# A decoder layer's quantised feed-forward: 12 of 32 recomputed hidden tiles go through DRAM instead

## What is computed

```python
def _quant_per_tensor(x):
    scale = jnp.maximum(jnp.max(jnp.abs(x)), MIN_RANGE) / QP
    return (_ste_round(x / scale), scale)
def _qlinear(x2d, w, b):
    xq, sx = _quant_per_tensor(x2d)
    wq, sw = _quant_per_tensor(w)
    return (jnp.matmul(xq, wq.T) + b[None, :]) * (sw * sx)
h = _qlinear(x, w1, b1)      # 8192 tokens x 1024
h = gelu(h)
o = _qlinear(h, w2, b2)      # 8192 tokens x 256
```

## Time and profile before

| | us |
|---|---|
| runs: median (lowest to highest of 3) | 1675.04 (1672.29 to 1675.15) |
| the profiled execution, its own time | 1671.48 |
| its span in the trace | 1669.4 |
| end of the last maximum of the first pass, in the span | 1561.66 |
| one pair of groups of the second pass | 23.93 |
| mean granted clock, share of full speed | 0.983 |

### The profile page before, as it was taken

The page is one execution under the profiler, slowest core; times in us unless marked ns, Lnnn a source line. Parts: engine busy times, 40 slices in busy tenths (PEclk is TensorE's granted clock), DMA queues, the critical chain, the costliest instruction groups (busy, mean ns, idle before and its releaser), DMA issues.

```text
span 1669.4 us, 51921 instructions
## 1 busy us (share of the span) xinstructions
PE 1573.6 (94%) x16058; PEld 1401.0 (84%) x16058; DVE 1461.2 (88%) x6184; ACT 1060.9 (64%) x2205; POOL 1051.2 (63%) x1168
## 2 busy tenths in 40 slices
PE   6799999999999999999999999999999999778898
PEld 5689999999999999999999999999999998644465
DVE  4889999999999999999999999999999996679876
ACT  4456666666666666666666666666666666469875
POOL 4557777777777777777777777777777776621000
PEclk9999999999999999999999999999999999789999
DMA  6000000000000000000000000000000000221155
GB/s 211 8 15 29 28 28 28 25 28 28 28 27 22 26 28 28 28 28 28 28 28 28 28 28 22 22 28 28 25 28 28 28 28 17 90 85 51 60 178 166
DMA packets 77732, 71.01 MB, mean 43 GB/s; under 512 B 6272, under 2 KB 77184, under 8 KB 77696
## 3 DMA queue, kind: packets, MB, share of 16 engines
q1 hardware_dynamic: 76736, 70.41, 13.4%
q10 hardware_dynamic: 960, 0.13, 0.1%
HBM read 45.36 MB, written 25.17 MB: 42 GB/s over the span
## 4 chain that ended last, share of the span: by engine, by line
PE 73%; DVE 14%; ACT 6%; issue 4%; POOL 1%; DMA 0%; ACTq 0%; DVEq 0%; SPq 0%; POOLq 0%
PE banks L111 21%; PE banks L112 18%; PE banks L113 18%; PE banks L868 5%; DVE tile_max L2010 4%; PE banks L848 3%; PE banks L892 3%; DVE xn L1241 3%; PE banks L1901 2%; ACT normed L1106 2%; DVE x L1390 1%; DVE ctx_t L1274 1%; ACT ctx_t L1076 1%; DVE kept L2022 1%; PE banks L747 1%
## 5 line engine op out<-in xcount | busy, mean ns | idle before, releaser
L589 POOL TENSOR_TENSOR shifted<-scores,score_max 128x512 f32<-128x512 f32 x256 | 266.9, 1043 | 200.6 <-DVE score_max L1286 159.9
L595 POOL TENSOR_TENSOR exp_t<-exp_copy,exp_t 128x512 f16<-128x512 f32 x256 | 302.5, 1182 | 60.6 <-ACT exp_copy L1091 60.6
L1286 DVE CUSTOM_DVE_ANT_0 scores<-banks,mask 128x128 f32<-128x128 f32 x1024 | 235.0, 286 | 11.6 <-issue 6.0
L1076 ACT ACTIVATE q_t<-banks 128x512 f16<-128x512 f32 x128 | 76.5, 598 | 224.0 <-PE banks L113 224.0
L581 POOL TENSOR_TENSOR v_nat<-kv_copy,v_nat 128x512 f16<-128x512 f32 x124 | 138.8, 1130 | 105.2 <-ACT kv_copy L1079 105.2
L111 PE MATMUL banks<-ctx_t,cross_Wk 128*128 128x256 f32 x512 | 154.7, 302 | 21.8 <-DVE ctx_t L1274 18.5
L1089 ACT ACTIVATE exp_t<-banks 128x512 f16<-128x512 f32 x256 | 155.9, 609 | 6.2 <-PE banks L113 3.8
L1091 ACT ACTIVATE exp_copy<-banks 128x512 f32<-128x512 f32 x256 | 158.6, 620 | 0.0
L868 PE MATMUL banks<-ident,shifted 128*128 128x128 f32 x1024 | 153.8, 279 | 3.9 <-POOL shifted L589 2.8
L111 PE MATMUL banks<-xn_t,cross_Wq 128*128 128x256 f32 x512 | 153.1, 299 | 2.7 <-POOL cross_Wo L269 1.6
L1079 ACT ACTIVATE kv_copy<-banks 128x512 f32<-128x512 f32 x248 | 150.9, 608 | 0.0
(11 more groups left out here) (261 smaller groups left out, 5661.8 us busy)
## 6 DMA issues: line engine op xcount, KB each, us to landing
x_in<-in_x_dram SPq DMA_DIRECT2D x32, 256.0 KB, 2.8
ctx_in<-in_ctx_dram SPq DMA_DIRECT2D x32, 256.0 KB, 2.7
x_residual<-x SPq DMA_DIRECT2D x64, 128.0 KB, 1.7
x_normalised<-normed SPq DMA_DIRECT2D x32, 256.0 KB, 2.1
shared<-x_normalised SPq DMA_DIRECT2D x8, 1024.0 KB, 5.3
shared<-x_residual SPq DMA_DIRECT2D x16, 512.0 KB, 3.8
out_dram<-shared SPq DMA_DIRECT2D x16, 512.0 KB, 2.9
mask<-in_fside_Bx1xSxS_dram SPq DMA_DIRECT2D x64, 64.0 KB, 1.8
```

What stands on the lines that cost most here:

```text
L589: pool.tensor_tensor(shifted[:, q % 2], scores[:, q % 2], score_max[:, q % 2, :].unsqueeze(2).to_broadcast([P, QUAD, P]), ALU.subtract).th ...
L595: pool.tensor_tensor(exp_t[:, q % 2, LO], exp_copy[:, q % 2], exp_t[:, q % 2, HI], ALU.subtract).then_inc(exp_split, 1)
L1076: op = act.activation(hilo(dst, *at)[HI], src, ACT.Copy)
L1286: op = dve.tensor_tensor_reduce(scores[:, q % 2, h, :], sc_bank(q)[:, tile(h)], mask[:, b, :], 1.0, NEG, ALU.add, ALU.max, score_max[:, q ...
```

## The change

Of the recomputed groups k = 3, 5 and 7 the rows t = 1, 3, 5, 7 (12 units, 6 MB) are no longer computed again. The first pass writes them to one of four tiles `held`, and SP stores each to DRAM. In the second pass, where the unit was due, PE does nothing for it, ACT issues the load of the unit into its slot in place of the Gelu, and `round_up` waits for the load. `held` lies in `shared` behind `x_load`: its four tiles cover rows 4 to 7 of the odd half of `h_q` and both `x_again`. So the first two reloads of residuals wait for all maxima and all stores, and so do the first takes of a recomputed group that write there (k = 1, row 4 on ACT and row 5 on DVE). The ring's tiles are now given in the order of the units that still pass through it, and the first three Gelus of the second pass wait for all 64 maxima, where each waited for the maximum of its own tile before.

```diff
@@ feed_forward: which tiles, and where they stand
+    HELD = 4
+    on_dram = lambda k, t: again(k) and k > 1 and t % 2 == 1
+    DRAM_UNITS = [(k, t) for k in range(GROUPS) for t in range(ET) if on_dram(k, t)]
+    AGAIN_UNITS = [(k, t) for k in range(GROUPS) for t in range(ET) if again(k) and not on_dram(k, t)]
+    first_pass = lambda k, t: SEQUENCE[k] * ET + t
+    held_of = {first_pass(*u): m for m, u in enumerate(DRAM_UNITS)}
+    ring_of = {first_pass(*u): m for m, u in enumerate(AGAIN_UNITS)}
+    unit_dram = nc.dram_tensor("hidden_units", (len(DRAM_UNITS), P, TOK), F32, kind="Internal").ap()
...
+    held = shared[:, SLOTS * GB * D:].rearrange("p (n s) -> p n s", n=HELD)
...
+    WAITS_FOR_DRAM = [next(u for u in all_units if u[0] == 1 and u[1] >= ET // 2 and on_act(*u) == act) for act in (True, False)]
...
         if j == 0:
-            at = (UNITS + t) % RING
-            return ring[:, at:at + 1, :] if t < RING else kept[:, t - RING:t - RING + 1, :]
+            return ring[:, t:t + 1, :] if t < RING else kept[:, t - RING:t - RING + 1, :]
...
+    def written(n):
+        if n in held_of:
+            return held[:, held_of[n] % HELD, :]
+        return ring[:, ring_of[n] % RING, :] if n in ring_of else kept[:, n, :]
+
+    def all_on_dram(eng):
+        for m in range(HELD):
+            eng.wait_ge(to_dram[m], 16 * (len(DRAM_UNITS) // HELD))
@@ sync: 12 stores, then the first reloads
+        for m, u in enumerate(DRAM_UNITS):
+            sp.wait_ge(h_ready, first_pass(*u) + 1)
+            sp.dma_start(unit_dram[m], held[:, m % HELD, :]).then_inc(to_dram[m % HELD], 16)
         sp.wait_ge(xt_full, PARTS * GROUPS)
         sp.wait_ge(b2_ready, 3)
+        sp.wait_ge(h_seen, UNITS)
+        all_on_dram(sp)
         reload(0)
@@ tensor: second pass
-            if due(step):
+            if due(step) and not on_dram(*due(step)):
                 k, t = due(step)
-                n = k // 2 * ET + t
+                n = AGAIN_UNITS.index((k, t))
@@ scalar: first pass
-                if g >= KEPT and n >= KEPT * ET + RING:
-                    act.wait_ge(h_seen, n - RING + 1)
-                gelu(kept[:, n, :] if g < KEPT else ring[:, n % RING, :], u1_bank(n), n, t, u_full, h_ready)
+                if n in held_of and held_of[n] >= HELD:
+                    m = held_of[n] - HELD
+                    act.wait_ge(to_dram[m % HELD], 16 * (m // HELD + 1))
+                    act.wait_ge(h_seen, first_pass(*DRAM_UNITS[m]) + 1)
+                if n in ring_of and ring_of[n] >= RING:
+                    act.wait_ge(h_seen, first_pass(*AGAIN_UNITS[ring_of[n] - RING]) + 1)
+                gelu(written(n), u1_bank(n), n, t, u_full, h_ready)
@@ scalar: take, and the second pass
+            if (k, t) == WAITS_FOR_DRAM[0]:
+                all_on_dram(act)
...
                 if j == 0 and t < RING:
-                    act.wait_ge(h_seen, UNITS - RING + t + 1)
+                    act.wait_ge(h_seen, UNITS)
...
-                gelu(unit(k, t)[:, 0, :], u2_bank(j * ET + t), j * ET + t, t, u2_full, h2_ready)
+                if on_dram(k, t):
+                    m = DRAM_UNITS.index((k, t))
+                    if m < HELD:
+                        act.wait_ge(to_dram[m], 16 * (len(DRAM_UNITS) // HELD))
+                    act.dma_start(unit(k, t)[:, 0, :], unit_dram[m]).then_inc(from_dram[m % HELD], 16)
+                else:
+                    n = AGAIN_UNITS.index((k, t))
+                    gelu(unit(k, t)[:, 0, :], u2_bank(n), n, t, u2_full, h2_ready)
@@ vector: round_up and take
-            if again(k):
-                dve.wait_ge(h2_ready, k // 2 * ET + t + 1)
+            if on_dram(k, t):
+                m = DRAM_UNITS.index((k, t))
+                dve.wait_ge(from_dram[m % HELD], 16 * (m // HELD + 1))
+            elif again(k):
+                dve.wait_ge(h2_ready, AGAIN_UNITS.index((k, t)) + 1)
...
+            if (k, t) == WAITS_FOR_DRAM[1]:
+                all_on_dram(dve)
```

More of the change, by code:

```diff
@@ L1663, in feed_forward @@
     again_loaded = [sem("again_loaded0"), sem("again_loaded1")]
+    to_dram = [sem(f"to_dram{n}") for n in range(HELD)]
+    from_dram = [sem(f"from_dram{n}") for n in range(HELD)]
     stored = [sem("stored0"), sem("stored1")]
@@ L2009, in vector @@
                 dve.wait_ge(h_ready, n + 1)
-                dve.tensor_reduce(tile_max[:, n:n + 1], kept[:, n, :] if g < KEPT else ring[:, n % RING, :], AX, ALU.max,
+                dve.tensor_reduce(tile_max[:, n:n + 1], written(n), AX, ALU.max,
                                   apply_absolute_value=True).then_inc(h_seen, 1)
```

## The result

| | before | after |
|---|---|---|
| median of 6 runs each, us | 1674.3 | 1680.88 |
| ratio, 95% interval | | 1.0041, 1.0028 to 1.0054 |
| span of the profiled execution, us | 1669.4 | 1678.9 |

The account below looks back on a forecast made before the run. DVE's work and its two waits for PE, a closed chain of 23.93 us per pair, bound the second pass. Shorter wait -1.44 plus clock falls +1.2 gave -0.24 us, from the median 1675.04 to 1674.8 us; range 1671 to 1680.

Parts of the forecast that it names:

- the closed chain of DVE's two blocks and two waits: Second pass, each pair of groups: DVE work 9.23, wait 2.48, work 9.78, wait 2.44, together 23.93 us.
- w1: DVE's wait for PE before a residual add, after O5's take: 2.48 to 2.00 us, -1.44 us over three pairs.
- PE's 10.3 us: Second pass: the 48 dropped matmuls of twelve units, mostly hidden beside DVE's work.
- ACT's 14.4: Second pass: the 12 dropped Gelus of 1203 ns, 14.4 us in all.
- The first pass carried the 12 stores: First pass: SP's stores of the held units land in time and cost 0.
- The loads were not late for the rounding: Second pass: unit loads, 3.8 us each, land before DVE rounds them, about 10 us after issue; cost 0.
- Blocks A and B: DVE's gapless work between its two waits in a second-pass pair: 9.23 and 9.78 us, unchanged by the change.
- the clock: Second pass, three pair boundaries: longer PE stops lower PE's clock at one or two, 0.8 us each, +1.2 us.
- PE's stop for E4-5: PE's idle time before E4's take at three pair boundaries: from 0.75 us to 2.1 to 2.4 us.
- The DMA engines: Second pass: the unit loads beside SP's stores and residual reloads delay nothing DVE needs; taken as 0.
- slack of 2.8 us: Time between a residual reload's landing and DVE's need of it: 3.24 us, 2.8 after the shorter wait.
- Rival (c): Second pass: loads crowd out residual reloads, each of 12 late by 1 us, +12, 1687 us; chance 0.07.

Follow-up runs that it names:

- e2: The changed kernel with only row t = 1 of groups k = 3, 5, 7 sent through DRAM, 3 units in place of 12: 1670.96 us, ratio 0.9986.
- e9: The changed kernel with only rows t = 1 and 5 sent through DRAM, 6 units in place of 12: 1670.98 us, ratio 0.9983.
- e11: e3 with PE still doing the matmuls of the 12 dropped units, into a bank nobody reads: 1670.68 us, ratio 0.9987.
- e10: The changed kernel with all 12 loads issued by SP in place of ACT, each behind a residual reload: 1686.93 us, ratio 1.0084.
- e1: The changed kernel without its 12 loads, stores and missing matmuls and Gelus kept: 1672.47 us, ratio 0.9992.
- e3: The changed kernel with residuals in four buffers in place of two from the fifth half on: 1672.51 us, ratio 0.9994.
- e5: The changed kernel with each unit laid out in DRAM in rows of 1 KB in place of 4 KB: 1677.91 us, ratio 1.0028.
- e4: The kernel before the change with residuals in four buffers from the fifth half on: 1672.51 us, ratio 0.9992.

## Why the prediction was wrong

The forecast was 1674.8 us, in a range of 1671 to 1680; 1680.88 was measured.

*Right.* The limit of the second pass is the closed chain of DVE's two blocks and two waits: the pairs of e2, e9 and e11, and the first pair of the change, are 23.47 to 23.53 us. Where the residual is in time w1 went from 2.48 to 2.01 (forecast 2.00), and nothing else of PE's 10.3 us or ACT's 14.4 came back. The first pass carried the 12 stores at no cost. The loads were not late for the rounding, but for 0.3 us once in e10. Blocks A and B together held 19.0 to 19.3 us of DVE in every kernel.

*Right in mechanism, off in size: the clock.* PE's stop for E4-5 became 2.06 us and the clock fell at one boundary of three in e1 and in e3, at none in the change's own three pairs. A fall cost 1.67 us, not 0.8. The price depends on how much of PE's work behind the stop it catches. In the row used for the estimate the clock was still 1.00 while 8 of the 12 matmuls started, and they took 1.82 us; in e1 it was 0.50 from 1622 on, when only 4 of the 16 had started, and they took 3.27. What is left of the forecast without the DMA term, -0.24 us, agrees with e1 and e3: 0.9992 and 0.9994, and both intervals hold 1.

*Wrong: the term "The DMA engines", taken as 0.* In the profiled execution this term came to 18.2 us of waits of DVE for residuals, in part in place of waits for PE, and to +4.15 and +4.31 us in two pairs. The prediction put one load in the way at 1.5 us, against a slack of 2.8 us. Two things failed. First the size: with loads in flight the median landing of a store went from 2.9 to 5.4 us (2.5, not 1.5) and that of a reload from 3.8 to 4.5, together 3.2 us; that alone is over the slack. Secondly, and this is what made 0.4 us into 4 per pair, the slack was counted from an issue time of the reload taken out of the trace of before. It is no constant. SP does not issue the next store before it has seen this one land and has issued the reload, so a late landing delays the other buffer's store, which then goes out beside the reload and lands later itself. The prediction asked what stands behind a wait for ACT and DVE, but not for SP's own wait for `stored`. The measure to take was SP's round, store to landing to reload: 3.2 us before, 5.4 to 7.7 in the two slow pairs, against 5.9 for a half. Rival (c) had this side of it right and its chance, 0.07, was far too low; its price of +12 was an upper figure for what came as +6.6.

The Trainium skill, DMA: Bandwidth & Descriptors (Issuing engines are not separate DMA queues), says that DMAs of different engines interleave on the same 16 engines. The runs are in line with it: stores landed late with the loads on ACT's queue as with the loads on SP's own (5.4 and 6.3 us, 2.9 without loads), and rows of 1 KB left it at 5.3. The Trainium skill, TensorE: Matmul & The Clock Gate (What's actually happening), ties the lower clock to an idle stretch; here it fell after stops of 2.06 us between two pieces of work, at some boundaries and not at others.

*Still open.* How often the clock falls after a stop of 2.06 us; why a load in flight costs a store 2.5 us, where 512 KB more in one transfer cost 1.5; and whether the rows of e5 save anything.

## What to carry to other kernels

Work that is taken off an engine pays only as far as it stands in the waits of the chain that sets the pace; here 0.5 of 3.4 us per pair did, and most of the rest came back only when the chain itself was opened by moving one instruction back in DVE's list. Before traffic is added beside a store and reload through a pair of buffers, compare the whole round (issue, landing, reissue by the queue that waits) with the time of one turn, not the landing with the slack of one transfer: a queue that waits for its own store turns a small delay into the next one's. Where tiles come free later in the kernel, as here, more buffers cost nothing that could be measured (e4) and remove that round (e3).

## What was not expected of the hardware

Reloads in flight for 5.6 us harm nobody while the DMA engines are 0.74 to 0.84 busy (e3), and stores that land in 5.4 us cost 4 us per pair while they are 0.70 busy (the change): the share in use says little about either. An issue of a DMA on ACT's queue took 0.33 us in this stage, against 0.49 at the start of the kernel. And 10.3 us more work on PE made a kernel no slower (e11); in its profiled execution the pairs were even and the granted clock stayed at 1.00 (2.4 GHz).
